# Two modulation blocks computed as columns, weights held and conditions streamed, in an adaLN transformer block on one core

## The chip, the cores and the metric

The kernel runs on one core of a Trainium2 chip. A core has five engines with instruction streams of their own: TensorE (PE in the profile; its weight loads are PEld), VectorE (DVE), ScalarE (ACT), GpSimd (POOL) and SyncE (SP, which here only issues DMA). They meet through semaphores. The metric is the device time in microseconds of one execution.

## The reference

One block with adaptive layer norm. A condition vector for each of two batches gives six modulation vectors of 512; the first two of them, `sa` and `ca`, are added to and multiplied with the normalised input ahead of the attention.

```python
mod = (silu(c) @ wmod).reshape(2, 6, 1, 512)      # c: (2, 512), wmod: (512, 3072)
sa, ca, ga, sb, cb, gb = (mod[:, i] for i in range(6))
ga, gb = sign(ga) * max(|ga|, 0.25), ...           # x: (2, 1024, 512)
h = layernorm(x) * (1 + ca) + sa
x = x + ga * attention(h)     # 32 query heads, 8 key/value heads of 128, rope, window of 128
h = layernorm(x) * (1 + cb) + sb
x = x + gb * ffn(h)           # silu gate, 512 wide, biases
```

## The kernel before, in words

All instructions of an engine run in the order in which its function writes them; waits on semaphores are written out by hand. The channels of a token lie on partitions where TensorE needs them, so the input is transposed on TensorE, tile by tile (128 tokens), and the modulation is then a scale and a shift per partition: `modT[:, kind, k, b]` holds for modulation `kind` (0 is `sa`, 1 is `1 + ca`) and channel block `k` (four of 128) one column per batch `b`.

Every matrix operand is split into two fp32r parts, a high one (ScalarE casts it) and a low one (VectorE subtracts), and a product is three matmuls of the parts (`mm3`, L276 to L278).

**The start.** SyncE and ScalarE issue the loads: the modulation weights `wm[0]` and `wm[1]` (512x512 float32 each) in halves of two channel blocks, with one semaphore a half (`s_wmk`), between them the first tiles of x into `y`, then the first weights `wk` and `wq` into the buffers `st`. `csil` is silu of the condition, transposed: 128 partitions x 4 blocks x 2 batches.

- TensorE: `mod_row(0)` and `mod_row(1)` hold the two columns of `csil` and stream 512 columns of weights, so each result is a row per batch, 2x512, in the banks `pTr` and `pAv`. Then `first_transpose(0)` and `(1)` turn two normalised tiles; `mod_columns(0)` turns the first row back into columns, four transposes into the bank `pXx`; `first_transpose(2)`, `(3)`, and `mod_columns(1)`.
- ScalarE: `row_copy(0, 0)` and `row_copy(1, 1)` copy the rows from PSUM into `crow`, which `mod_columns` reads. Behind them in its stream stand two weight casts (`split_weight`), then `first_act` of tiles 0, 2 and 3, which applies `modT`.
- VectorE: statistics and normalisation of tiles 0 to 3 (`ln_stats`, L965 to L969, and `ln_apply`, L977), `split_first(0)` and `(1)` (L1036), each of which waits for its ScalarE cast, `mod_out(0)` and `(1)` (L1090, L1092), which wait until both blocks' columns are there and write `modT`, then `first_tile` of tiles 1 (which it scales itself, L991), 0, 2 and 3: a cast (L999) and a subtraction (L1001) into `hT`.
- TensorE starts the projections when tiles 1 and 0 are in `hT` (`l_chunk0`): K and the first query head, each in two halves of 256 tokens, then the other heads and V, with the transposes of tiles 4 to 6 between them.

From there VectorE, ScalarE and GpSimd apply rope and the splits in a relay (`swap`, `rope_cos`, `rope_sin`, `rope_sum`, `rope_hi`, `rope_lo`); the other four modulation blocks are still computed as rows later on, and the loop over heads and tiles follows, with the feed-forward part at the end.

Of the kernel before, what the change touches and what calls it, by code (L numbers as in the profile page):

```python
# [24 lines left out]
P = 128  # L25
# [46 lines left out]
def adaln_block(nc, x, wq, wk, wv, wo, w12, b12, w3, b3, cond, wmod, cos, sin, x1_spill, out):  # L72
    B, SEQ, D = x.shape
# [4 lines left out]
    KT = D // P  # L78
# [7 lines left out]
    with ExitStack() as ctx:  # L86
        def sb(name, shape, dt):
            return ctx.enter_context(nc.sbuf_tensor(name, shape, dt))

        def sem(name):  # L90
            return ctx.enter_context(nc.semaphore(name))
# [8 lines left out]
        def over(name, region, offset, shape, dt):  # L100
            return nc.alloc_sbuf_tensor_at(name, shape, dt, offset=base[region] + offset)
# [23 lines left out]
        csil = sb("csil", [P, KT, B], F32)  # L125
# [10 lines left out]
        wm = [over(f"wm{i}", r, o, [P, KT, 512], F32) for i, (r, o) in enumerate(  # L136
            [("qT0", 0), ("qT0", 8192), ("wos", 0), ("qT1", 0), ("qT1", 8192), ("wos", 8192)])]
# [15 lines left out]
        pTr, pAv, pOp, pXx, pP0, pP1 = (ctx.enter_context(nc.psum_tensor(n, [P, 512], F32))  # L153
                                        for n in ("pTr", "pAv", "pOp", "pXx", "pP0", "pP1"))
# [6 lines left out]
        s_wm = [sem(f"s_wm{i}") for i in range(6)]  # L161
        s_wmk = [[sem(f"s_wmk{i}{k}") for k in range(2)] for i in range(2)]


        s_cT, s_cact, s_cdve, s_row, s_rowc, s_mod, s_modT, s_gdve, s_bias = (sem(n) for n in (
            "s_cT", "s_cact", "s_cdve", "s_row", "s_rowc", "s_mod", "s_modT", "s_gdve", "s_bias"))
# [37 lines left out]
        def l_acted(L):  # L204

            return L if L else 1
# [66 lines left out]
        def _(pe):  # L273
# [93 lines left out]
            def first_transpose(L):  # L367

                pe.wait_ge(l_norm, L + 1)
                if L in (4, 5):  # L370
                    pe.wait_ge(s_rowc, L - 3)
                if L == 6:
                    pe.wait_ge(s_modT, 1)
                if L == 7:
                    pe.wait_ge(l_act, l_acted(4))
                for k in range(KT):
                    last = nc.tensor.transpose(ln_banks[L][:, k * P:(k + 1) * P], y[:, L, k * P:(k + 1) * P], ident[:])
                last.then_inc(l_tr, 1)
# [58 lines left out]
            def mod_row(r):  # L437

                w = ROW_BLOCK[r]
                if r >= 2:  # L440
                    pe.wait_ge(s_wm[w], 16)
                if r == 3:
                    pe.wait_ge(l_act, l_acted(5))
                if r == 4:
                    pe.wait_ge(s_rowc, 3)
                if r == 5:
                    pe.wait_ge(s_modT, 2)
                for k in range(KT):
                    if r < 2 and k % 2 == 0:
                        pe.wait_ge(s_wmk[r][k // 2], 16)  # L450
                    last = nc.tensor.matmul(row_banks[r], csil[:, k, :], wm[w][:, k, :],
                                            start=(k == 0), stop=(k == KT - 1))
                last.then_inc(s_row, 1)

            def mod_columns(kind):

                pe.wait_ge(s_rowc, kind + 1)
                if kind == 2:
                    pe.wait_ge(j_done, 6)
                for k in range(KT):  # L460
                    at = 8 * kind + 2 * k
                    last = nc.tensor.transpose(pXx[:, at:at + B], crow[:, kind % 2, k * P:(k + 1) * P], ident[0:B, 0:B])
                last.then_inc(s_mod, 1)
# [2 lines left out]
            pe.wait_ge(s_c, 16)  # L466
            nc.tensor.transpose(pXx[:, 0:B * KT], c8[:], ident[0:B * KT, 0:B * KT]).then_inc(s_cT, 1)
            pe.wait_ge(s_cdve, 3)
            mod_row(0)
            mod_row(1)  # L470
            first_transpose(0)
            first_transpose(1)
            mod_columns(0)
            first_transpose(2)
            first_transpose(3)
            mod_columns(1)
            f0 = Frame(pe, 0)

            def project_half(name, half):
# [141 lines left out]
        def _(act):  # L621
            def split_weight(f, dst, W, slot):

                f.wait(w_in[slot], 32, 16 * (W // 5 + 1))
                nc.scalar.copy(dst, st[:, slot, :]).then_inc(w_hi, 1)
# [43 lines left out]
            def v_hi(f, ch, v):  # L669

                f.wait(v_turn, PER_V, v)
                nc.scalar.copy(kv[:, 0, 1, ch * CT:(ch + 1) * CT], pXx[:]).then_inc(v_half, 1)
# [34 lines left out]
            def first_act(L):  # L707

                act.wait_ge(l_tr, L + 1)
                for k in range(KT):  # L710
                    last = nc.scalar.activation(y[:, L, k * P:(k + 1) * P], ln_banks[L][:, k * P:(k + 1) * P],
                                                ACT.Identity, bias=modT[:, 0, k, 0:1], scale=modT[:, 1, k, 0:1])
                last.then_inc(l_act, 1)
# [27 lines left out]
            def unit_step(f, u, b, jobs, prev=True, prev2=True, split=True):  # L741
                if u == 2:

                    f.wait(u_scores, PER_U, u + 1)
                    splits(f, u, b)
                if prev2:
                    result_hi(f, u - 2)
                if prev:
                    p_hi(f, u - 1)
                exps(f, u)  # L750
                jobs()
                if split and u in (3, 4, 5):
                    splits(f, u, b)
# [6 lines left out]
                                 ).then_inc(s_cact, 1)  # L760

            def row_copy(r, slot):
                act.wait_ge(s_row, r + 1)
                nc.scalar.copy(crow[:, slot, :], row_banks[r]).then_inc(s_rowc, 1)

            f0 = Frame(act, 0)
            row_copy(0, 0)
            row_copy(1, 1)
            split_weight(f0, wp[:, 0, 0, :], 0, 0)
            split_weight(f0, wp[:, 0, 1, :], 1, 1)  # L770
            act.wait_ge(s_modT, 1)
# [19 lines left out]
            for b in range(B):  # L791
                s0 = b * NKV
                f = Frame(act, s0)

                def first_jobs(u):
                    if b == 0 and u == 1:
                        act.wait_ge(s_row, 5)
                    if b == 0 and u == 0:
                        first_act(7)
                        row_copy(3, 1)  # L800
                        v_hi(f, 0, 1)
                    jobs_act(f, u, b)
                for u in range(2):
                    unit_step(f, u, b, lambda: first_jobs(u), prev=s0 > 0 or u > 0, prev2=s0 > 0)
                if b == 0:
                    act.wait_ge(s_row, 6)
                else:
                    act.wait_ge(s_modT, 2)
                with nc.scalar.Fori(s0, s0 + NKV - 1) as s:
                    f = Frame(act, s, regs, s0)  # L810
                    for u in range(2, NT + 2):
                        unit_step(f, u, b, lambda: jobs_act(f, u, b, js=u // NT))
                        if u == 6:
                            side_act(f, b)
                f = Frame(act, s0 + NKV - 1)
                for u in range(2, NT):
                    def jobs():
                        if b == 0 or u < CH:
                            jobs_act(f, u, b)
                        elif u < NT - 1:  # L820
                            weight_tr_act(4 * (u - CH)), weight_tr_act(4 * (u - CH) + 1)
                    unit_step(f, u, b, jobs, split=b == 0)
                    if u == 6:
                        side_act(f, b)
                    if b == 1 and CH <= u < NT - 1:
                        weight_tr_act(4 * (u - CH) + 2), weight_tr_act(4 * (u - CH) + 3)
# [33 lines left out]
        def _(dve):  # L860
# [245 lines left out]
            def gate_row(gate):  # L1106

                bank, g = row_banks[4 + gate], grow[:, gate, :]
                dve.wait_ge(s_row, gate + 5)
                nc.vector.tensor_scalar(g, bank, 0.0, 0.5, ALU.is_ge, ALU.subtract).then_inc(s_gdve, 1)  # L1110
                dve.wait_ge(s_gdve, 3 * gate + 1)
                nc.vector.scalar_tensor_tensor(out=gmag[:], in0=g, scalar=4.0, in1=bank, op0=ALU.mult,
                                               op1=ALU.mult).then_inc(s_gdve, 1)
                dve.wait_ge(s_gdve, 3 * gate + 2)
                nc.vector.scalar_tensor_tensor(out=g, in0=gmag[:], scalar=2 * MIN_GATE, in1=g, op0=ALU.max,
                                               op1=ALU.mult).then_inc(s_gdve, 1)
# [119 lines left out]
            for h in range(2):  # L1236
                n = slice(256 * h, 256 * h + 256)
# [387 lines left out]
```

## Time and profile before

| | |
|---|---|
| median of 3 runs | 1498.3 us (1497.09, 1498.3, 1499.03) |
| profiled execution | 1499.11 us, span 1497.3 us |
| TensorE busy | 1474.5 us, 98% of the span |
| VectorE, GpSimd, ScalarE busy | 1102.8, 863.2, 823.0 us |
| mean granted clock of TensorE | 0.997 |
| first projection starts | 21.57 us after the span's start |

The busy share is over the whole span; the first 60 us look different from the rest and are read on their own. The granted clock is a share of 2.4 GHz: 1.00 is 2.4 GHz, 0.50 is 1.2 GHz. Times within the trace count from the span's first instruction.

### The profile page before, as it was taken

The numbers are of one execution on the slowest core, as the hardware profiler recorded it, in microseconds if no ns is written. First come the engines' busy times: TensorE is split into PE (matmuls) and PEld (weight loads), VectorE is DVE, ScalarE is ACT, GpSimd is POOL, SyncE is SP. The second block draws the span as 40 slices with busy tenths as digits, with TensorE's granted clock in tenths as the row PEclk, the third lists the DMA queues.
The fourth block names the chain that finished last, engine by engine and source line by source line (L and its number), as shares of the span: only waits on it lengthen the run. The fifth ranks groups of instructions, "written<-read, shape, count | busy, mean of one in ns | idle before, by whom it ended". The sixth has DMA issues, their size and how long they took to land.

```text
span 1497.3 us, 27356 instructions
## 1 busy us (share of the span) xinstructions
PE 1474.5 (98%) x7589; PEld 1227.1 (82%) x7589; DVE 1102.8 (74%) x1852; ACT 823.0 (55%) x2183; POOL 863.2 (58%) x887
## 2 busy tenths in 40 slices
PE   7899999999999999999999999999999999999999
PEld 4578888888888888888888888888888888877887
DVE  6687786877787878788787878787877868783542
ACT  3465655656555656555565655565665556552331
POOL 2356466656565556669855646655664665676333
PEclk9999999999999999999999999999999999999999
DMA  9011110110201111324302020111111101153001
GB/s 317 21 37 57 36 56 28 38 53 7 84 7 56 35 56 35 127 62 128 99 27 66 7 82 9 56 35 56 35 56 35 56 28 35 64 183 127 28 29 57
DMA packets 99216, 90.20 MB, mean 60 GB/s; under 512 B 5466, under 2 KB 73314, under 8 KB 99174
## 3 DMA queue, kind: packets, MB, share of 16 engines
q1 hardware_dynamic: 98582, 88.50, 18.8%
q10 hardware_dynamic: 432, 0.66, 0.1%
q0 software_dynamic: 160, 0.52, 0.1%
q8 instruction: 21, 0.34, 0.1%
q14 instruction: 21, 0.17, 0.0%
HBM read 74.98 MB, written 14.69 MB: 60 GB/s over the span
## 4 chain that ended last, share of the span: by engine, by line
PE 91%; DVE 4%; POOL 2%; issue 1%; ACT 1%; DMA 0%; DVEq 0%; POOLq 0%; ACTq 0%
PE pP L276 11%; PE pP L278 11%; PE pP L277 11%; PE pOp L276 8%; PE pOp L278 8%; PE pOp L277 8%; PE pS L278 4%; PE pS L277 4%; PE pAv L276 4%; PE pS L276 4%; PE pAv L278 4%; PE pAv L277 4%; PE pTr L286 3%; PE pXx L355 1%; POOL pm L1256 1%
## 5 line engine op out<-in xcount | busy, mean ns | idle before, releaser
L1256 POOL TENSOR_SCALAR_AFFINE_SELECT pm<-pT 128x512 fp32r<-128x512 f32 x480 | 393.3, 852 | 474.4 <-DVE pT L868 474.2
L276 PE MATMUL pP<-hT,wp 128*128 128x512 f32 (+1 forms) x776 | 315.1, 406 | 4.7 <-DVE hT L1001 4.0
L278 PE MATMUL pP<-hT,wp 128*128 128x512 f32 (+1 forms) x776 | 303.7, 391 | 0.0
L277 PE MATMUL pP<-hT,wp 128*128 128x512 f32 (+1 forms) x776 | 302.8, 390 | 0.0
L630 ACT CAST oT<-pAv 128x512 fp32r<-128x512 f32 x128 | 74.8, 585 | 280.9 <-PE pAv L278 280.9
L1269 POOL TENSOR_TENSOR rB<-rB,tab 128x512 f32<-128x512 f32 x160 | 218.4, 1377 | 17.3 <-ACT rB L653 17.3
L642 ACT ACTIVATE pr<-pS,nb 128x128 f32<-128x128 f32 x512 | 181.4, 371 | 64.3 <-DVE nb L888 64.3
L898 DVE TENSOR_TENSOR rA<-pP,tab 128x512 f32<-128x512 f32 x160 | 110.2, 689 | 130.8 <-ACT rB L653 130.8
L276 PE MATMUL pOp<-wos,oT 128*128 128x512 f32 x512 | 201.4, 393 | 4.0 <-DVE oT L863 3.8
L278 PE MATMUL pOp<-wos,oT 128*128 128x512 f32 x512 | 199.5, 390 | 0.0
L277 PE MATMUL pOp<-wos,oT 128*128 128x512 f32 x512 | 199.4, 389 | 0.0
L278 PEld LDWEIGHTS pP<-hT,wp 128*128 128x128 f32 x776 | 147.4, 190 | 32.0
L276 PEld LDWEIGHTS pP<-hT,wp 128*128 128x128 f32 x776 | 147.6, 190 | 30.7 <-DVE hT L1001 4.1
L277 PEld LDWEIGHTS pP<-hT,wp 128*128 128x128 f32 x776 | 148.1, 191 | 26.6
L915 DVE TENSOR_TENSOR qT<-rA,qT 128x512 fp32r<-128x512 f32 x128 | 135.3, 1075 | 19.3 <-ACT qT L662 19.3
L1263 POOL TENSOR_TENSOR pr<-pr,rs 128x512 f32<-128x512 f32 x128 | 139.3, 1088 | 15.7 <-DVE rs L893 15.7
L276 PE MATMUL pS<-kv,qT 128*128 128x192 f32 (+2 forms) x512 | 141.4, 276 | 0.1
L278 PE MATMUL pS<-kv,qT 128*128 128x192 f32 (+2 forms) x512 | 140.8, 275 | 0.0
L277 PE MATMUL pS<-kv,qT 128*128 128x192 f32 (+2 forms) x512 | 140.2, 274 | 0.0
L904 DVE TENSOR_TENSOR rA<-rA,rB 128x512 f32<-128x512 f32 x160 | 132.5, 859 | 0.0
L652 ACT COPY rB<-pP 64x512 f32<-64x512 f32 x160 | 93.5, 584 | 62.5 <-PE pP L278 60.1
L276 PEld LDWEIGHTS pOp<-wos,oT 128*128 128x128 f32 x512 | 96.1, 188 | 30.0 <-issue 5.7
(196 smaller groups left out, 3008.6 us busy)
## 6 DMA issues: line engine op xcount, KB each, us to landing
st<-in_L_attn_wq_dram SPq DMA_DIRECT2D x64, 256.0 KB, 3.6
st<-in_L_attn_wo_dram SPq DMA_DIRECT2D x64, 256.0 KB, 3.8
h_dram<-hs SPq DMA_DIRECT2D x16, 512.0 KB, 3.9
st<-in_L_attn_wk_dram SPq DMA_DIRECT2D x16, 256.0 KB, 4.0
st<-in_L_attn_wv_dram SPq DMA_DIRECT2D x16, 256.0 KB, 2.8
wm<-in_L_wmod_dram SPq DMA_DIRECT2D x4, 1024.0 KB, 10.1
xin<-in_L_attn_x_dram SPq DMA_DIRECT2D x16, 256.0 KB, 3.0
qT<-h_dram SPq DMA_DIRECT2D x2, 2048.0 KB, 10.2
```

The lines of the kernel that those rows point to most:

```text
L276: nc.tensor.matmul(o, hi_l, hi_r, start=start, stop=False, skip_group_check=True)
L277: nc.tensor.matmul(o, hi_l, lo_r, start=False, stop=False, skip_group_check=True)
L278: return nc.tensor.matmul(o, lo_l, hi_r, start=False, stop=stop, skip_group_check=True)
L630: nc.scalar.copy(oT[:, 0].rearrange("p h q -> p (h q)"), pAv[:]).then_inc(u_ohi, 1)
L642: last = nc.scalar.activation(pr[:, u % 2, i, :], pS[:, at:at + P], ACT.Exp, bias=nb[:, u % 2, i:i + 1], scale=SCALE, accum_out=sums[:, u ...
L652: nc.scalar.copy(rB[0:64, r, :], pP[j % 2][64:128, :])
L898: nc.vector.tensor_tensor(rA[:, j % 3, :], pP[j % 2][:], tab[:, 0, ch * CT:(ch + 1) * CT], ALU.mult).then_inc(r_cos, 1)
L904: nc.vector.tensor_tensor(rA[:, j % 3, :], rA[:, j % 3, :], rB[:, j % 3, :], ALU.add).then_inc(r_sum, 1)
L915: nc.vector.tensor_tensor(dst, src, hi, ALU.subtract).then_inc(j_done, 1)
L1256: last = nc.gpsimd.affine_select(out=pm[:, own, part], in_=pT[:, part], compare_op=op, fill=0.0, base=0, pattern=[[0, G], [sign, P]], chan ...
L1263: nc.gpsimd.tensor_tensor(pr[:, u % 2], pr[:, u % 2], rs[:, u % 2, :].unsqueeze(2).to_broadcast([P, G, P]), ALU.mult).then_inc(u_norm, 1)
L1269: nc.gpsimd.tensor_tensor(rB[:, j % 3, :], rB[:, j % 3, :], tab[:, 1, ch * CT:(ch + 1) * CT], ALU.mult).then_inc(r_sin, 1)
```

## The change

`mod_row` no longer computes blocks 0 and 1. `mod_direct` does: for each of the four input blocks k and four output blocks n it holds a 128x128 piece of the modulation weights and streams the two columns of `csil`, accumulating over k straight into the columns of `pXx` that `mod_out` reads. The rows, their two copies on ScalarE and the eight column transposes go away. Both blocks are computed ahead of the four tile transposes, which were mixed with the column transposes before. The remaining waits on row counts are renumbered, and the waits of tiles 4 and 5 on the row copies go, since the banks `pTr` and `pAv` no longer hold rows 0 and 1.

```diff
             def first_transpose(L):
 
                 pe.wait_ge(l_norm, L + 1)
-                if L in (4, 5):
-                    pe.wait_ge(s_rowc, L - 3)
                 if L == 6:
                     pe.wait_ge(s_modT, 1)
...
             def mod_row(r):
 
                 w = ROW_BLOCK[r]
-                if r >= 2:
-                    pe.wait_ge(s_wm[w], 16)
+                pe.wait_ge(s_wm[w], 16)
                 if r == 3:
                     pe.wait_ge(l_act, l_acted(5))
                 if r == 4:
-                    pe.wait_ge(s_rowc, 3)
+                    pe.wait_ge(s_rowc, 1)
                 if r == 5:
                     pe.wait_ge(s_modT, 2)
                 for k in range(KT):
-                    if r < 2 and k % 2 == 0:
-                        pe.wait_ge(s_wmk[r][k // 2], 16)
                     last = nc.tensor.matmul(row_banks[r], csil[:, k, :], wm[w][:, k, :],
                                             start=(k == 0), stop=(k == KT - 1))
                 last.then_inc(s_row, 1)
 
+            def mod_direct(kind):
+
+                for k in range(KT):
+                    if k % 2 == 0:
+                        pe.wait_ge(s_wmk[kind][k // 2], 16)
+                    for n in range(KT):
+                        at = 8 * kind + 2 * n
+                        last = nc.tensor.matmul(pXx[:, at:at + B], wm[kind][:, k, n * P:(n + 1) * P], csil[:, k, :],
+                                                start=(k == 0 and n == 0), stop=(k == KT - 1),
+                                                skip_group_check=True)
+                last.then_inc(s_mod, 1)
+
             def mod_columns(kind):
 
-                pe.wait_ge(s_rowc, kind + 1)
+                pe.wait_ge(s_rowc, kind - 1)
...
             pe.wait_ge(s_cdve, 3)
-            mod_row(0)
-            mod_row(1)
-            first_transpose(0)
-            first_transpose(1)
-            mod_columns(0)
-            first_transpose(2)
-            first_transpose(3)
-            mod_columns(1)
+            mod_direct(0)
+            mod_direct(1)
+            for L in range(4):
+                first_transpose(L)
             f0 = Frame(pe, 0)
...
             def row_copy(r, slot):
-                act.wait_ge(s_row, r + 1)
+                act.wait_ge(s_row, r - 1)
                 nc.scalar.copy(crow[:, slot, :], row_banks[r]).then_inc(s_rowc, 1)
 
             f0 = Frame(act, 0)
-            row_copy(0, 0)
-            row_copy(1, 1)
             split_weight(f0, wp[:, 0, 0, :], 0, 0)
             split_weight(f0, wp[:, 0, 1, :], 1, 1)
             act.wait_ge(s_modT, 1)
```

On TensorE, at the start of the program, behind the transposition of the condition, the difference reads as follows (`wm_49` and `wm_50` are the two weight blocks; the operand named first behind the arrow is the one streamed for the rows, `wm`, and the one held is `csil`; the shape is that of the output).

```order
-L451 MATMUL pTr<-wm_49,csil 2x512 x4
-L451 MATMUL pAv<-wm_50,csil 2x512 x4
-L377 MATMUL pP<-ident,y 128x128 x8
-L462 MATMUL pXx<-ident,crow 128x2 x4
-L377 MATMUL pS<-ident,y 128x128 x8
-L462 MATMUL pXx<-ident,crow 128x2 x4
+L457 MATMUL pXx<-csil,wm_49 128x2 x16
+L457 MATMUL pXx<-csil,wm_50 128x2 x16
+L375 MATMUL pP<-ident,y 128x128 x8
+L375 MATMUL pS<-ident,y 128x128 x8
```

Eight row products and eight column transposes become 32 products of two columns, and the sixteen tile transposes (four tiles) stand behind them in one piece.

On ScalarE, from the start of the program to the first application of `modT`, this stood before:

```order
L759 ACTIVATE cT<-pXx 128x8
L764 COPY crow<-pTr 2x512
L764 COPY crow<-pAv 2x512
L625 CAST wp<-st 128x512 x2
L711 ACTIVATE y<-pP,modT 128x128 x4
L711 ACTIVATE y<-pS,modT 128x128 x8
L625 CAST wp<-st 128x512
```

and this stands there now:

```order
L762 ACTIVATE cT<-pXx 128x8
L628 CAST wp<-st 128x512 x2
L714 ACTIVATE y<-pP,modT 128x128 x4
L714 ACTIVATE y<-pS,modT 128x128 x8
L628 CAST wp<-st 128x512
```

The two weight casts no longer stand behind the row copies. The orders of VectorE, GpSimd and SyncE are as they were.

## Rows read from the trace of the kernel before

**Rows 1.** The page: busy times, and the chain's shares by engine
```profile
PE 1474.5 (98%) x7589; PEld 1227.1 (82%) x7589; DVE 1102.8 (74%) x1852; ACT 823.0 (55%) x2183; POOL 863.2 (58%) x887
...
PE 91%; DVE 4%; POOL 2%; issue 1%; ACT 1%; DMA 0%; DVEq 0%; POOLq 0%; ACTq 0%
```

**Rows 2.** A window of the body: busy by engine, clock, DMA share, GB/s
```profile
800.00:1200.00 400.00, 400.00 (x2104) 338.51 (x2103) 310.12 (x523) 236.67 (x641) 233.82 (x241) 1.00 0.14 43
```

**Rows 3.** The chain of waits, 0 to 60 us: start, us, what
```profile
0.82 4.06 DMA wm<-in_L_wmod_dram
...
5.01 6.42 PE pTr L451 x8
11.44 3.43 PE pAv L451 x8
14.87 1.03 PE pP L377 x8
...
17.25 0.35 PE pXx L462 x4
...
17.90 1.38 DVE y L991 x4
...
21.57 0.58 PE pP L276
...
22.37 0.21 PE pP L278
...
28.64 0.12 PE pP L277
```

**Rows 4.** Windows of the start, same columns (busy in turn of PE, PEld, DVE, ACT, POOL)
```profile
40.40:44.30 3.90, 0.00 (x0) 0.00 (x0) 3.83 (x8) 1.48 (x4) 2.26 (x2) 1.00 0.22 67
...
44.80:48.20 3.40, 3.40 (x11) 2.64 (x10) 3.33 (x7) 0.62 (x1) 2.24 (x2) 0.51 0.00 0
...
21.50:27.70 6.20, 6.12 (x28) 6.13 (x29) 5.55 (x14) 1.20 (x3) 1.33 (x2) 0.50 1.05 386
```

**Rows 5.** Line L451, 0 to 30 us: ns min/median/max, first and last start
```profile
L451 PEld LDWEIGHTS pTr<-wm,csil x8: 80/129/129, 5.0 to 10.1; 128*2 128x2 f32 x8
L451 PE MATMUL pTr<-wm,csil x8: 593/1061/1061, 5.0 to 10.8; 128*2 128x512 f32 x8
L451 PEld LDWEIGHTS pAv<-wm,csil x8: 85/85/86, 10.8 to 13.9; 128*2 128x2 f32 x8
L451 PE MATMUL pAv<-wm,csil x8: 592/592/592, 11.3 to 14.3; 128*2 128x512 f32 x8
```

**Rows 6.** Timeline of TensorE's loads at the first column transposes
```profile
15.83 0.32 PEld L462 LDWEIGHTS pXx<-ident,crow 2*128 2x128 f32 x4 [0.17 <-issue]
```

**Rows 7.** Line L462, 0 to 30 us
```profile
L462 PEld LDWEIGHTS pXx<-ident,crow x8: 133/136/138, 15.8 to 17.4; 2*128 2x128 f32 x8
L462 PE MATMUL pXx<-ident,crow x8: 195/196/218, 15.8 to 17.4; 2*128 2x2 f32 x8
```

**Rows 8.** DMA issues at 2.84, 4.5 and 5.0 us: size, us to landing
```profile
wm<-in_L_wmod_dram SPq DMA_DIRECT2D x1, 512.0 KB, 7.5
...
st<-in_L_attn_wk_dram SPq DMA_DIRECT2D x1, 256.0 KB, 8.1
...
st<-in_L_attn_wq_dram SPq DMA_DIRECT2D x1, 256.0 KB, 8.5
```

**Rows 9.** Timelines of VectorE and of ScalarE, 14 to 19 us
```profile
14.45 0.55 DVE L977 TENSOR_SCALAR y<-y,mv 128x512 f32<-128x512 f32 x1 [0.44 <-POOL mv L1281]
16.04 1.29 DVE L1036 TENSOR_TENSOR wp<-st,wp 128x512 fp32r<-128x512 f32 x2 [1.04 <-ACT wp L625]
17.63 0.17 DVE L1090 COPY modT<-pXx 128x8 f32<-128x8 f32 x1 [0.29 <-PE pXx L462]
...
15.39 1.13 ACT L625 CAST wp<-st 128x512 fp32r<-128x512 f32 x2
...
19.28 2.90 ACT L711 ACTIVATE y<-pS,modT 128x128 f32<-128x128 f32 x8
```

More of the change, by code:

```diff
@@ L796, in first_jobs @@
                     if b == 0 and u == 1:
-                        act.wait_ge(s_row, 5)
+                        act.wait_ge(s_row, 3)
                     if b == 0 and u == 0:
@@ L805, in _ @@
                 if b == 0:
-                    act.wait_ge(s_row, 6)
+                    act.wait_ge(s_row, 4)
                 else:
@@ L1108, in gate_row @@
                 bank, g = row_banks[4 + gate], grow[:, gate, :]
-                dve.wait_ge(s_row, gate + 5)
+                dve.wait_ge(s_row, gate + 3)
                 nc.vector.tensor_scalar(g, bank, 0.0, 0.5, ALU.is_ge, ALU.subtract).then_inc(s_gdve, 1)
```

## The prediction

> **What bounds the kernel now.** I began with the page: TensorE is busy for 98% of the span and carries 91% of the chain that ended last, VectorE only 4% [rows 1]. The windows over the body say the same: from 60 us on TensorE has no hole worth naming [rows 2]. So nothing in the body changes, and whatever the start gains or loses in reaching that body reaches the end one for one. The change touches only the first 18 us.
>
> Next the chain of waits at the start [rows 3]. It runs from the landing of the first half of the first modulation block (0.82 + 4.06 = 4.9) over the two row products on TensorE (6.42 and 3.43 us), the transposes of four tiles with the eight small column transposes between them (to 17.25 + 0.35 = 17.60), and then VectorE: shift and scale of tile 1 from 17.90, and the splitting of tiles 1 and 0. There the first projection starts, at 21.57. Behind it TensorE works until the relay of ScalarE, VectorE and GpSimd through rope makes it wait once more, 40.4 to 44.3 [rows 4], and then it is the bound.
>
> **What the change does to TensorE.** Removed: 16 instructions of 512 streamed columns and 8 column transposes. The rows cost 6.42 + 3.43 = 9.85 us, the columns 2 x 0.35 = 0.70 [rows 3]. The first eight row instructions were at TensorE's lower level (1061 ns each, 1.2 GHz), the second eight at the higher (592 ns, 2.4 GHz) [rows 5]. Added: 2 blocks x 4 k x 4 n = 32 products. The trace shows each float32 product as two instructions (x8 where the program has four) [rows 5], so 64 pairs of a 128-column weight load and a 2-column stream.
>
> No row has that very pair. The nearest is the column transpose: 128 columns held, 2 streamed, at the high level. Four loads are busy for 0.32 us together [rows 6], each 0.136 [rows 7], so they start (0.32 - 0.136) / 3 = 0.061 us apart; on the chain a group of four takes 0.35, 0.088 each [rows 3]. At the low level I allow twice either: 0.12 to 0.18 us. Below, the bound is 0.061; above, it is the whole load without any overlap. That load at the low level: a 2-column load takes 85 ns high and 129 low [rows 5], a 128-column one 136 high [rows 7], so 126 columns cost 51 ns high, 102 low, together 0.231. I take 0.14, between the two readings of the nearest row, and the low level throughout, since nothing shows whether this work raises the clock. Then the blocks last 64 x 0.14 = 9.0 us, from 5.0 to 14.0.
>
> The weights arrive in time: the last half block is issued at about 2.8 and takes 7.5 us, so it lands at about 10.3 [rows 8], when three quarters of the pairs (5.0 + 48 x 0.14 = 11.7) aren't yet done. With pairs at 0.061 this landing would set the end instead: 10.3 + 16 x 0.061 = 11.3.
>
> Behind the blocks stand the four tile transposes. Eight took 1.03 us at the high level [rows 3], so at the low level tiles 0 and 1 are through at 14.0 + 2.1 = 16.1.
>
> **What waits for it.** On ScalarE the copy of the second row, which waited for the product's end, held the first weight split back to 15.39 [rows 9]. Both copies go. The split then waits for its data: wk was issued at about 4.5 and takes 8.1, so it lands at 12.6, wq at 5.0 + 8.5 = 13.5 [rows 8]. The splits take 1.13 us together [rows 9], so the second is done by about 14.1.
>
> VectorE's order isn't changed. It normalises tile 3 until 14.45 + 0.55 = 15.00, then idled 1.04 us for the split, did its two halves in 1.29 us, idled 0.29 for the columns and wrote modT [rows 9]. Now the first idle goes (the splits are there at 14.1), and the second too (the blocks end at 14.0). So VectorE: 15.0 + 0.02, + 1.29 = 16.3, and with the two small operations at the old spacing (17.63 to 17.90, 0.27) the shift of tile 1 starts at 16.6 instead of 17.90. TensorE has tile 1 ready at 16.1. **The gain is 1.04 + 0.29 = 1.3 us**, not the several us that TensorE saves: VectorE's tile statistics and splits are the next thing late, and hide the rest. ScalarE starts tile 0 at the same moment. Tiles 2 and 3 are transposed by 14.0 + 4.1 = 18.1, before ScalarE comes to tile 3, two tiles of 1.45 us after 16.6 [rows 9].
>
> Everything behind moves by 1.3 us: the projection starts at about 20.3. The loads that SyncE issues when VectorE frees a weight buffer come 1 us earlier, and TensorE waits for none of them: its one long wait behind the projection's start is that for VectorE until 44.3. The removed waits of tiles 4 and 5 cost nothing now, for those tiles stand behind the projections. Were VectorE's work out of the way, TensorE would set the start: tile 1 is through at 16.1, so at these prices there are only 0.5 us more behind it.
>
> **The clock.** It was low over the first 6.2 us of the projection, after TensorE had stood idle from 17.60 to 21.57 [rows 3, 4]; it was low again from 44.8 to 48.2, behind the idle 3.9 us that ended at 44.3 [rows 4]. Low, a projection step is 0.21 us, high 0.12 [rows 3]. In the new order the idle time before the projection is longer, so it starts low again; I take the same low stretch. If it lasted only 3.4 us, as the other did, 2.8 us fewer would be worth 2.8 x (1 - 0.12 / 0.21) = 1.2 us; if the second fall didn't come, 3.4 x (1 - 0.12 / 0.21) = 1.5.
>
> **Sum.** The profiled execution took 1499.1 us (its span of 1497.3 and 1.8 around it); 1499.1 - 1.3 = 1497.8. It was 0.8 above the median of 1498.3, and 1499.03 and 1497.09 are among the three runs: executions differ by as much as the change is worth. Against the median I forecast 1497.0.
>
> **The rivals.**
> *A, the pairs don't overlap (slower).* A load can't start under the last matmul, and the clock stays low: 64 x 0.231 = 14.8, blocks to 19.8, tiles 0 and 1 to 21.9, shift of tile 1 at 22.0 instead of 17.90: +4.1 us, 1502.4. For it: the loads are 128 columns wide and nothing else is in the stream, and the high level came only after 5.8 us of wide products, 5.0 to 10.8 [rows 5]. Against it: the 0.061 spacing of loads 0.136 long [rows 6, 7]. It decides from a pair of (17.9 + 3.0 - 2.1 - 5.0) / 64 = 0.216 us on. Chance 0.08.
>
> *B, pairs of 0.15 to 0.21 us.* From (16.6 - 2.1 - 5.0) / 64 = 0.149 on TensorE is late again. At 0.175 the start is 5.0 + 11.2 + 2.1 = 18.3, a loss of 0.4; at 0.20 a loss of 2.0. Time 1497.5 to 1501, chance 0.2.
>
> *C, the clock gives back as well.* 1.3 + 1.2 + 1.5 = 4.0 us: 1494.3. For it: both falls follow idle stretches of about 3.9 us, and both shift. Against it: neither idle stretch gets shorter. Chance 0.12 for a gain of over 3 us, which needs most of both.
>
> *D, loads wait for the matmul's full duration.* Each pair would then take 0.136 + 0.196 = 0.332 us even at the high level [rows 7], 64 of them 21.2 us; blocks to 26.2, shift of tile 1 at 27.3, +9.4 us, 1507.7. Against it: four such pairs take 0.35 us on the chain [rows 3], where it would give 1.33. Chance 0.02.
> The Trainium skill ("TensorE: Matmul & The Clock Gate", Part 3, "The mechanism") states this rule: a weight load overlaps a matmul in flight only if the two use different row groups, and all loads here use all rows. The trace of the column transposes does not agree with it.
>
> *E, the forecast*, 0.58.
>
> **Numbers.** A change of under 0.2% (3.0 us) is about what a measurement of this kernel can't tell from none. Faster by more: C, 0.12. Slower by more: A and D, 0.10. Within: 0.78. The range leaves out D, A and the far end of C: with B's upper end and the spread of the runs, 1494.6 to 1499.9.
>
> **What the changed profile would show.** 64 load and stream pairs on pXx between 5.0 and about 14, 0.12 to 0.18 us apart, with at most a short wait for the last half block; no row copies before the first split, which starts at about 12.6; no idle time of VectorE between 15.0 and modT at about 16.4; the first projection at about 20.3; TensorE's second long wait ending at about 43.0; the body unchanged. It is wrong if modT waits for TensorE, if tile 1's shift waits for its transpose, or if the first projection's low stretch differs by several us from 6.2.

## The result, and the profile after

The changed kernel is slower: 1501.21 us median (1500.17 to 1502.51, 14 runs) against 1498.22 (1497.09 to 1499.03, 14 runs), a ratio of 1.002 with the 95% interval 1.0013 to 1.0027. The forecast was 1497.0, within 1494.6 to 1499.9. Run again later beside other kernels it gave 1501.86 against 1498.74, 1.0023 (1.0013 to 1.0032). One execution of all, among the eleven with the third block's row product in the idle time, took 5973.57 us and is left out of that run's median and ratio.

The page of the changed kernel, in the lines that answer to [rows 1]:

```profile
span 1499.7 us, 27432 instructions
...
PE 1479.1 (99%) x7629; PEld 1240.0 (83%) x7629; DVE 1103.1 (74%) x1852; ACT 822.2 (55%) x2181; POOL 863.2 (58%) x887
```

The page says that TensorE's busy time grew by 4.6 us, though the change was to relieve it, and that VectorE's did not change. Where it grew stands in the chain of waits (start, us, what), beside [rows 3]:

```profile
0.82 3.78 DMA wm<-in_L_wmod_dram
4.73 13.78 PE pXx L457 x64
18.52 1.82 PE pP L375 x8
20.44 1.38 DVE y L992 x4
...
24.11 0.58 PE pP L276
24.70 0.21 PE pP L277
...
31.23 0.58 ACT rB L655
...
46.64 0.91 PE pXx L375 x4
```

Two row products of 9.85 us became 64 pairs of 13.78 us, and eight tile transposes that took 1.03 us take 1.82. Tile 1's shift starts at 20.44 instead of 17.90, 2.5 us late, the projection at 24.11 instead of 21.57, the copy of the K bank (ScalarE, L655, the first work on the projection's result) at 31.23 instead of 28.91, and the span is 2.4 us longer. So the start's shift did reach the end nearly one for one.

The products' line and the tile transposes' line (ns min/median/max, first and last start), beside [rows 5] and [rows 7]:

```profile
L457 PEld LDWEIGHTS pXx<-csil,wm x64: 287/333/333, 4.7 to 18.1; 128*128 128x128 f32 x64
L457 PE MATMUL pXx<-csil,wm x64: 343/353/353, 4.7 to 18.2; 128*128 128x2 f32 x64
```

```profile
L375 PEld LDWEIGHTS pP<-ident,y x8: 224/230/370, 18.2 to 19.7; 128*128 128x128 f32 x8
L375 PE MATMUL pP<-ident,y x8: 421/421/454, 18.4 to 19.9; 128*128 128x128 f32 x8
```

The loads are 333 ns long but for the first. 64 of them follow each other every (13.73 - 0.333) / 63 = 0.213 us, 13.73 being their joint busy time in the timeline, so each starts under the one before. That is 256 cycles at 1.2 GHz: two cycles for each of the 128 held columns. The transpose's load, also of 128 columns, is 230 ns here, 103 less: about one cycle a column less. Both lines are at the low level from the first to the last instruction, to nearly 22 us, where the kernel before had risen at 10.8.

The trace of the kernel before has loads of 128 columns for products too, which [rows 5] to [rows 7] don't show. These are the projection's at the low level and at the high one, and two successive loads of the scores (start, us), at the high level, with 64 columns streamed behind each:

```profile
L276 PEld LDWEIGHTS pP<-hT,wp x6: 330/330/330, 22.2 to 25.4; 128*128 128x128 f32 x6
...
L276 PEld LDWEIGHTS pP<-hT,wp x9: 186/187/192, 29.0 to 34.7; 128*128 128x128 f32 x9
...
52.88 0.19 PEld L277 LDWEIGHTS pS<-kv,qT 128*128 128x128 f32 x1
52.99 0.19 PEld L278 LDWEIGHTS pS<-kv,qT 128*128 128x128 f32 x1
```

They belong to products of fp32r parts, one instruction a product, but the load is as long as that of the new pairs (330 against 333 ns), and the scores' loads start 0.11 us apart at the high level, which is half of 0.213.

What waited for TensorE, on VectorE and on ScalarE, beside [rows 9]:

```profile
14.80 1.28 DVE L1037 TENSOR_TENSOR wp<-st,wp 128x512 fp32r<-128x512 f32 x2
18.55 0.17 DVE L1091 COPY modT<-pXx 128x8 f32<-128x8 f32 x1 [2.46 <-PE pXx L457]
18.64 0.16 DVE L1093 TENSOR_SCALAR modT<-pXx 128x8 f32<-128x8 f32 x1
20.44 1.37 DVE L992 TENSOR_SCALAR y<-pP,modT 128x128 f32<-128x128 f32 x4 [1.65 <-PE pP L375]
```

```profile
12.50 0.62 ACT L628 CAST wp<-st 128x512 fp32r<-128x512 f32 x1 [9.10 <-DMA st<-in_L_attn_wk_dram]
13.37 0.62 ACT L628 CAST wp<-st 128x512 fp32r<-128x512 f32 x1 [0.25 <-DMA st<-in_L_attn_wq_dram]
19.57 1.50 ACT L714 ACTIVATE y<-pP,modT 128x128 f32<-128x128 f32 x4 [5.59 <-PE pP L375]
```

The casts moved up to the landing of their weights, as forecast, and VectorE's splits run on from its last normalisation. Then VectorE waits twice for TensorE: 2.46 us for the blocks, 1.65 us for tile 1. Both waits were to be nothing.

One reading needs care. A window of the changed kernel over its first projection (busy times of PE, PEld, DVE, ACT, POOL, then granted clock, DMA, GB/s):

```profile
24.10:30.20 6.10, 6.08 (x30) 6.09 (x31) 5.45 (x13) 0.52 (x2) 1.33 (x2) 1.00 1.05 386
```

The column says 1.00, but the steps in it are 0.21 us apart, the low level's distance; so it does in the first microseconds of every kernel here. At the start the level is read from the durations.

### The profile page after: what moved, and what is told of

It is laid out like the page before. It is cut to its first block, busy times and chain, and to the rows that moved or that the text cites. A ratio compares the mean times of both kernels' runs of the same rounds, so it can differ in the third digit from the quotient of the medians.

```text
span 1499.7 us, 27432 instructions
## 1 busy us (share of the span) xinstructions
PE 1479.1 (99%) x7629; PEld 1240.0 (83%) x7629; DVE 1103.1 (74%) x1852; ACT 822.2 (55%) x2181; POOL 863.2 (58%) x887
## 4 chain that ended last, share of the span: by engine, by line
PE 91%; DVE 4%; POOL 2%; issue 1%; ACT 1%; DMA 0%; DVEq 0%; POOLq 0%; ACTq 0%
PE pP L276 11%; PE pP L278 11%; PE pP L277 11%; PE pOp L276 8%; PE pOp L278 8%; PE pOp L277 8%; PE pS L278 4%; PE pS L277 4%; PE pAv L276 4%; PE pS L276 4%; PE pAv L277 4%; PE pAv L278 4%; PE pTr L286 3%; PE pXx L457 1%; PE pXx L355 1%
## 5 line engine op out<-in xcount | busy, mean ns | idle before, releaser
L655 ACT COPY rB<-pP 64x512 f32<-64x512 f32 x160 | 93.4, 584 | 62.9 <-PE pP L278 60.5
## 6 DMA issues: line engine op xcount, KB each, us to landing
wm<-in_L_wmod_dram SPq DMA_DIRECT2D x4, 1024.0 KB, 10.8
```

What stands on the lines that cost most here:

```text
L655: nc.scalar.copy(rB[0:64, r, :], pP[j % 2][64:128, :])
```

## The experiments

Two questions were open: what a pair costs, and why the clock stayed low. Each run below is compared with the kernel before on the same chip.

**64 columns streamed.** The loads are the same, but more columns go through them. The results go to the banks `pTr` and `pAv`, from which `mod_out` reads the first two of each 64 columns, and tiles 4 and 5 wait for `modT`, because they use the same banks; of the edit only the product is shown.

```diff
-                        at = 8 * kind + 2 * n
-                        last = nc.tensor.matmul(pXx[:, at:at + B], wm[kind][:, k, n * P:(n + 1) * P], csil[:, k, :],
+                        last = nc.tensor.matmul((pTr, pAv)[kind][:, 64 * n:64 * (n + 1)],
+                                                wm[kind][:, k, n * P:(n + 1) * P],
+                                                csil[:, k, :].unsqueeze(1).to_broadcast([P, 32, B]),
```

> Each of the 64 loads is followed by a stream of 64 columns (the two condition columns repeated 32 times, the copies going to spare columns of the banks pTr and pAv) in place of 2; the loads, their order and the result are the same. Theory 1 (the loss is the clock: two-column streams leave TensorE at its low level, where a load pair costs 0.215 us): the clock rises at about 10.5 to 11, as it did under the row products; from there a pair takes about half, 0.11 us, the blocks end at about 14.5 instead of 18.5, the tile transposes are at the high level, VectorE's shift of tile 1 starts at about 16.6 to 17, and the kernel takes 1496 to 1498 us, 3 to 4 less than the changed kernel. Rival 2 (a pair costs 0.215 us whatever the clock, say in the sequencer): the pairs stay at 0.215 us, the end at 18.5, and only the transposes get faster: 1500 to 1501. Rival 3 (the clock doesn't rise on this work, however wide): as the changed kernel or slower, 1501 to 1502.

Measured: 1501.98 us against 1498.74, 1.0024 (1.0014 to 1.0034). The loads of both blocks:

```profile
L456 PEld LDWEIGHTS pTr<-csil,wm x32: 289/333/337, 5.1 to 11.7; 128*128 128x128 f32 x32
L456 PEld LDWEIGHTS pAv<-csil,wm x32: 333/333/333, 11.9 to 18.5; 128*128 128x128 f32 x32
```

Nothing moved: the loads are at the low level to the end of the blocks, at the same distance. The 62 extra columns cost no time, so the stream lies wholly beside the loads. Theory 1 as I had put it (a wider stream brings the clock up) failed here. Whether the stream was still too small, or the clock wasn't to be moved, this run can't say; and as the clock never rose, rival 2 (0.215 us at any clock) isn't tested by it either.

**128 columns streamed.** The same edit with 128 for 64 and 64 for 32.

> As the run with 64 streamed columns, now 128 (the two condition columns 64 times over), so that the stream takes as long as the load, 256 cycles each. With 64 columns the pairs stayed at 0.216 us and the clock stayed low. If it is the share of time in which columns stream that raises the clock (in the row products they stream nearly all the time), it now rises at about 10.5 to 11, the later pairs take half, the blocks end at about 14.7, and the kernel takes 1496 to 1498 us. Rival (load and stream of such a product don't overlap): pairs of 0.32 to 0.43 us, blocks beyond 25, 1508 or more. Rival (it stays low whatever is streamed): as the changed kernel, 1501.

Measured: 1497.28 us against 1498.24, 0.9992 (0.9983 to 1.0001). Loads, streams, and VectorE's start:

```profile
L456 PEld LDWEIGHTS pTr<-csil,wm x32: 190/333/333, 4.9 to 10.6; 128*128 128x128 f32 x32
L456 PE MATMUL pTr<-csil,wm x32: 272/421/553, 4.9 to 10.8; 128*128 128x128 f32 x32
L456 PEld LDWEIGHTS pAv<-csil,wm x32: 191/191/192, 10.8 to 14.2; 128*128 128x128 f32 x32
```

```profile
14.85 1.29 DVE L1038 TENSOR_TENSOR wp<-st,wp 128x512 fp32r<-128x512 f32 x2
16.05 0.16 DVE L1095 COPY modT<-pTr 128x8 f32<-128x8 f32 x1
16.13 0.16 DVE L1097 TENSOR_SCALAR modT<-pAv 128x8 f32<-128x8 f32 x1
16.32 1.37 DVE L993 TENSOR_SCALAR y<-pP,modT 128x128 f32<-128x128 f32 x4
```

The first block's loads are 333 ns long but for the last ones, the second's all 191: the high level came at 9.7, near the end of the first block. In the second block 32 loads are busy for 3.65 us (the timeline's figure), so they start (3.65 - 0.191) / 31 = 0.112 us apart, half of 0.213 and a few ns, so a price of 0.215 us at any clock is out. The last load ends at 14.4, no wait is left between VectorE's splits and tile 1's shift, and that starts at 16.32, 4.1 us ahead of the changed kernel and 1.6 ahead of the kernel before. With this one number altered, the start of the changed kernel goes as the prediction said. The gain on the kernel before lies just inside what the runs can't tell from none; the interval doesn't touch that of the changed kernel (1.0013 to 1.0032).

**64 columns held.** Half of each output block is left out of the computation, so the result is incomplete and only the trace counts. One more transposition of the condition stands ahead of it and writes columns 8 to 15 of `pXx`.

```diff
-                        last = nc.tensor.matmul(pXx[:, at:at + B], wm[kind][:, k, n * P:(n + 1) * P], csil[:, k, :],
+                        last = nc.tensor.matmul(pXx[0:64, at:at + B], wm[kind][:, k, n * P:n * P + 64], csil[:, k, :],
...
+            nc.tensor.transpose(pXx[:, B * KT:2 * B * KT], c8[:], ident[0:B * KT, 0:B * KT])
             nc.tensor.transpose(pXx[:, 0:B * KT], c8[:], ident[0:B * KT, 0:B * KT]).then_inc(s_cT, 1)
```

> Each product of the two blocks holds 64 columns of weights instead of 128 (the upper half of each output block is left out of the computation). Theory 1 (the pair is the load, two cycles per held column at 1.2 GHz: 128 x 2 / 1.2 = 213 ns): a pair takes about 0.11 us at the low level and the blocks are bound by the landing of the last half block at 10.3, ending at about 12. Rival 2 (a fixed cost per pair): pairs stay at 0.215 us and the blocks end at about 18.5.

Measured: 1497.36 us, a single execution. From the timeline:

```profile
4.63 1.78 PEld L457 LDWEIGHTS pXx<-csil,wm 128*64 128x64 f32 x16 [1.99 <-DVE swapped L1077]
...
7.03 5.19 PEld L457 LDWEIGHTS pXx<-csil,wm 128*64 128x64 f32 x48 [0.62 <-DMA wm<-in_L_wmod_dram]
```

The median load is 227 ns, so 48 of them start (5.19 - 0.227) / 47 = 0.106 us apart, half of 0.213. A pair costs its held columns, two cycles each at 1.2 GHz, and next to nothing besides; a fixed cost is out. The wait in it is for the second half block's weights, not for the last as expected: the last 48 loads run on without one. The clock stayed low under the blocks here too, and it didn't matter: they end at 12.2, tile 1's shift starts at 16.11. So halving the load and doubling the clock are worth about the same, and either makes VectorE the one to wait for.

**Block 0 as a row, block 1 directly.** The counts that the waits on rows and their copies use are set to match; that part of the edit isn't shown.

```diff
-            mod_direct(0)
+            mod_row(0)
             mod_direct(1)
+            mod_columns(0)
```

> Block 0 as a row (its copy and its four column transposes with it), block 1 directly, then the transposes of tiles 0 to 3. The row product brings the clock up by 10.5 to 11, so block 1's pairs run at the high level. If the pair is the load of 256 cycles, they take 0.107 us there (32 in 3.4 us, ending at about 14.7), the tile transposes are at the high level, VectorE runs through from 15.0, tile 1's shift starts at about 16.7, and the kernel gains the 1.3 us that the prediction forecast: 1497. If the pair costs 0.215 us at any clock, block 1 ends at 18.2 and the kernel takes 1500 or more.

Measured: 1498.43 us against 1498.24, 1.0000 (0.9991 to 1.0009). Windows over block 1 and over the tile transposes (columns as above), and VectorE's start:

```profile
12.50:13.50 1.00, 1.00 (x11) 1.00 (x11) 0.93 (x5) 0.64 (x2) 0.45 (x1) 1.00 1.07 361
...
14.50:15.00 0.50, 0.50 (x4) 0.50 (x3) 0.50 (x2) 0.00 (x0) 0.00 (x0) 0.50 1.04 382
...
17.00:18.00 1.00, 1.00 (x6) 1.00 (x6) 0.00 (x0) 0.48 (x2) 0.00 (x0) 0.50 1.09 348
```

```profile
14.91 1.28 DVE L1044 TENSOR_TENSOR wp<-st,wp 128x512 fp32r<-128x512 f32 x2
16.40 0.17 DVE L1098 COPY modT<-pXx 128x8 f32<-128x8 f32 x1 [0.20 <-PE pXx L474]
...
18.39 1.36 DVE L999 TENSOR_SCALAR y<-pP,modT 128x128 f32<-128x128 f32 x4 [1.74 <-PE pP L377]
```

The pair is about 0.11 us at the high level, as expected, for the first 25 loads (starts from 11.5 to 14.2). Then came what I had not expected: the granted clock fell to 0.50 by 14.5, while TensorE was busy all through the windows around it, with nothing but these pairs since 11.5. The tile transposes ran low, tile 1's shift waited 1.74 us for them, and the gain was gone. So it isn't only that this work can fail to raise the clock; here the clock fell under it. The place is seen in one trace, but the mean granted clock of all eleven executions (0.994 to 0.995) is below the 0.997 that nearly all of the kernel before show.

**Tile 0 between the blocks.**

```diff
             mod_direct(0)
+            first_transpose(0)
             mod_direct(1)
-            for L in range(4):
+            for L in range(1, 4):
```

> The changed kernel with tile 0's transposes between the two blocks, the rest of the order as it is. If the order matters only by the time that TensorE needs behind the blocks for tiles 0 and 1 (0.23 us a transpose at the low level, 1.9 us for eight), tile 1 is through 0.9 us earlier only if its own transposes come first; here the last block ends 0.9 us later (19.4) and tile 1 at the same time as before, about 20.4: no change, 1501. Rival (VectorE could start 1 us earlier because tile 0 is off the path): 1500.

Measured: 1502.14 us against 1498.74, 1.0024 (1.0014 to 1.0033).

```profile
20.71 1.37 DVE L993 TENSOR_SCALAR y<-pP,modT 128x128 f32<-128x128 f32 x4 [0.80 <-PE pP L375]
```

Tile 1's shift starts no earlier, as expected; this order gives nothing, and TensorE's own work sets the start. Moving tile 1's transposes themselves ahead of the last pairs was not tried. This trace shows one thing more, which bears on the clock: the projection's steps are at the high level from its first at 24.39, though TensorE had stood idle for 2.1 us before and no filler was there, and the K bank's copy starts at 29.00. The execution took 1501.32 us all the same; the low level came later and lasted from 43.3 to 50.1.

**The kernel before, with casts and columns first.** Rows as they were.

```diff
             row_copy(0, 0)
-            row_copy(1, 1)
             split_weight(f0, wp[:, 0, 0, :], 0, 0)
             split_weight(f0, wp[:, 0, 1, :], 1, 1)
+            row_copy(1, 1)
...
             mod_columns(0)
+            mod_columns(1)
             first_transpose(2)
             first_transpose(3)
-            mod_columns(1)
```

> The kernel before, rows and all, with two moves: ScalarE's two weight casts ahead of the second row's copy, and the second block's column transposes ahead of the transposes of tiles 2 and 3. If what the start waits for in the kernel before is VectorE behind those casts and columns, VectorE runs through from 15.0, modT is there at about 16.7 in place of 17.9 and the kernel gains 1.0 to 1.3 us: about 1497.1. Rival (the gain is lost again, in the clock's low stretch or in the relay to 44 us): 1498.2, as before.

Measured: 1497.6 us against 1498.74, 0.9995 (0.9986 to 1.0004). Tile 1's shift starts at 16.17:

```profile
14.70 1.28 DVE L1036 TENSOR_TENSOR wp<-st,wp 128x512 fp32r<-128x512 f32 x2
15.90 0.16 DVE L1090 COPY modT<-pXx 128x8 f32<-128x8 f32 x1
...
16.17 1.36 DVE L991 TENSOR_SCALAR y<-pP,modT 128x128 f32<-128x128 f32 x4
```

No wait is printed between VectorE's splits and tile 1's shift, as with 128 streamed columns. All that the change could have given at this place in the trace comes from the order of ScalarE's and TensorE's instructions, with the rows kept. The median is 1.1 us lower, in line with it, but the interval takes in no gain at all.

**The third block's row product in TensorE's idle time,** on top of the last one.

```diff
+                if name == "Q3":
+                    mod_row(2)
                 if name != "V":
                     first_transpose(2 + j)
-            mod_row(2)
```

> The rows version with casts and columns first (its profile's TensorE idle from about 38.7 to 42.6), and the row product of the third block (3.5 us) moved from behind the V projection into that idle time, ahead of tile 6's transposes. If TensorE's own work bounds everything behind the idle time, 3.5 us go, and if the fall of the clock behind it comes from the idle time, another 1.5: 1492 to 1494 us. Rival (something else releases the scores at 51, or the block's weights are late): 1496 to 1497.5.

Measured: 1499.0 us (median of ten) against 1498.24, 1.0006 (0.9997 to 1.0016). The 1492 to 1494 expected are missed: no gain, and if anything a loss. Windows:

```profile
40.00:44.00 4.00, 3.59 (x16) 1.99 (x14) 3.93 (x8) 1.78 (x3) 2.03 (x2) 1.00 0.00 0
44.00:48.00 4.00, 1.30 (x6) 0.75 (x4) 3.32 (x6) 1.89 (x4) 1.80 (x2) 0.98 0.00 0
48.00:52.00 4.00, 3.29 (x16) 3.29 (x16) 2.92 (x6) 4.00 (x12) 0.00 (x0) 0.50 0.01 2
```

and, in the chain of waits, the last link of the relay ahead of TensorE:

```profile
47.96 0.70 DVE qT L916
```

The idle time moved from before 44 to behind it: the scores wait for the relay, which VectorE's rope of the last query head ends only at 48.7. They do start earlier, at 48.71 against 51.06 in the run that this one builds on, but the clock was low behind this idle time too, to 54.7, where the other trace is at the high level from 46.5 on, and the lead was gone. In the kernel before, the relay ends at 51.2 and TensorE's row product stands from 49.25 to 52.77, so it covered that wait. The prediction's view that TensorE is the bound from 44.3 on therefore held only because the row product stood where it did.

**The filler, and two last versions.** Eight row products into a bank that nobody reads, behind tile 3's transposes, first on top of the last run, then on the version with 128 streamed columns and on the rows version with casts and columns first:

```diff
+            for k in range(KT):
+                nc.tensor.matmul(row_banks[2], csil[:, k, :], wm[1][:, k, :], start=(k == 0), stop=(k == KT - 1))
             f0 = Frame(pe, 0)
```

> The same, and eight row products of 512 columns whose result nobody reads put between tile 3's transposes and the first projection, about 16.5 to 19.9, where TensorE was idle. If the low level in the first projection (0.21 us a step instead of 0.12, over some 6 us) comes from that idle time, the K bank is done 2 to 2.8 us earlier and the kernel gains up to 2.4 us more: 1490 to 1492. Rival (the relay behind it is bound by VectorE's own work, or the clock falls anyway): as the run without the filler.

> The direct products with 128 streamed columns, and the eight unread row products of 512 columns behind tile 3's transposes, about 16.3 to 19.8. Theory (the first projection's low level comes from TensorE's idle time before it): the clock is high when the projection starts at about 20, the K bank is done some 2 us earlier than without the filler (26.1), and the kernel gains about 2 us on the 128-column run, 3 on the kernel before: 0.998, or 1495 us where the kernel before takes 1498. Rival (the relay of VectorE behind it takes up the gain): 0.9992, as without the filler.

> The rows version with casts and columns first, with the same filler and without the move of the third block's row product. If that move was what cost the earlier run its gain (1 to 2 us lost against the version without it), this one takes 0.998 of the kernel before, level with the direct version with filler, since both start tile 1's shift at about 16.2 to 16.3: how the columns are computed makes no difference once VectorE is the one to wait for. Rival (the direct version is better by the copies and column transposes that it saves): this one is over 1 us slower than the direct version with filler.

> The changed kernel once more, beside the others on this chip: 1.002 of the kernel before, the 64 pairs 0.215 us apart at the low level to 18.5, and tile 1's shift at 20.4.

Measured: on top of the moved row product 1496.4 against 1498.24, 0.9990 (0.9981 to 0.9999), where 1490 to 1492 had been expected; with 128 streamed columns 1495.55 against 1498.74, 0.9983 (0.9974 to 0.9992); with rows 1495.98, 0.9983 (0.9974 to 0.9992). The changed kernel, on the chip of the last two: 1501.86, 1.0023. Windows over the place of the filler and over the projection, first without it (128 columns), then with it:

```profile
16.40:19.90 3.50, 0.00 (x0) 0.00 (x0) 3.40 (x9) 3.50 (x11) 0.00 (x0) 1.00 1.14 323
20.00:26.80 6.80, 6.80 (x44) 6.80 (x45) 5.48 (x13) 1.84 (x5) 1.33 (x2) 0.75 1.06 380
```

```profile
16.30:20.00 3.70, 3.70 (x15) 1.10 (x13) 3.56 (x11) 3.48 (x11) 0.00 (x0) 1.00 1.15 324
20.00:26.80 6.80, 6.52 (x50) 5.82 (x48) 6.08 (x15) 2.98 (x7) 1.75 (x3) 1.00 1.06 380
```

With the filler the clock stays high through the projection, in all three traces that have one, and the copy of the K bank starts 4.6 us behind the projection's start instead of 6.1 (25.12 - 20.50 against 26.08 - 20.00). What the filler itself gives is seen best in the two runs on the same chip that differ in nothing else: 1499.0 us without and 1496.4 with it, on top of the moved row product, and nine of the ten executions without it took longer than the longest with it. So the relay doesn't take up all of the gain. With 128 streamed columns the filler's share is less sure: the two ratios to the kernel before, 0.9992 and 0.9983, have intervals that overlap, and the K bank was done 1.0 us earlier, not 2. Both last versions beat both kernels, by 3.2 and 2.8 us on the kernel before and by about 6 on the changed one, and they are level with each other, as expected, with tile 1's shift at 16.52 and 16.70: rows or columns makes no difference once VectorE is the one to wait for.

The changed kernel's second trace, with the start of the projection in two windows:

```profile
5.14 13.79 PE pXx L457 x64
...
20.86 1.38 DVE y L992 x4
```

```profile
24.50:26.00 1.50, 1.47 (x12) 1.47 (x13) 1.43 (x4) 0.55 (x2) 0.00 (x0) 1.00 1.05 386
26.10:29.30 3.20, 3.20 (x17) 3.20 (x16) 3.06 (x9) 0.00 (x0) 0.56 (x2) 0.50 1.06 387
```

The pairs cost the same to a hundredth, and tile 1's shift is 0.4 us later because the blocks' start is. But the projection began at the high level here and was low from 26.0 to 29.4 only, 3.4 us instead of nearly 6. How much of the projection runs low thus differs between executions of one kernel. Idle time ahead of the projection isn't enough for a low start, by this trace and by that with tile 0 between the blocks; without the idle time none of three was low.

## Why the prediction was wrong

- **The step that failed: "I take 0.14, between the two readings of the nearest row".** The pair costs 0.213 us at the low level. The nearest row was that of a transpose, and a transpose's load takes about one cycle a held column where that of a product takes two. The same row fits for how loads follow each other (0.061 us for loads of 136 ns) and misleads on how long each holds the path. The trace of before has rows for the price that the working didn't use: the projection's loads of 128 columns last 330 ns low and 187 high, and the scores' loads start 0.11 us apart high, twice of which is 0.22. That a float32 product's load would match one of fp32r parts could only be assumed then; the changed kernel shows it. The rows used for rival A give the length too, once a load of a product stands in for that of the transpose: 187 - 85 = 102 ns for 126 columns more at the high level, so 204 at the low, where the prediction had 51 and 102; with the 129 of the short load that makes 333 ns, the length measured.
- **The low level throughout the blocks** was assumed and was so. The rest of the formula holds: 4.73 + 13.78 for the blocks and 1.82 for tiles 0 and 1 give 20.3, and tile 1's shift started at 20.44. With 0.213 in place of 0.14, rival B's working gives 5.0 + 13.6 + 2.1 = 20.7, 2.8 us behind the 17.90 of before.
- **Rivals.** The outcome stands between B (0.15 to 0.21) and A (0.216 on), for a reason that is neither's: the loads do overlap, spaced 0.213 and 333 ns long, but each costs about twice what the transpose's does. That B's span of prices happened to reach to 0.21 was luck: its working had no reason for the doubling. B's own time ran to 1501, and the range was closed at 1499.9 although it claims to take in B's upper end; that sum was wrong, and the result of 1501.21 lies just above B's end. Rival D is out for these pairs as well: the matmuls take 353 ns each and don't add to the pair. With that the rule of the Trainium skill that the prediction names there ("TensorE: Matmul & The Clock Gate", Part 3, "The mechanism") doesn't hold here. The pairs are the better witness: the prediction says that all loads use all rows, but those of the column transposes have two ([rows 7]), and only the 64 pairs' loads have all 128.
- **What hides the rest.** That VectorE would be the next to wait for, and the gain of 1.3 us with it, was right as a mechanism: with 128 streamed columns, and with 64 held, VectorE shows no wait for TensorE there and tile 1's shift starts 1.6 and 1.8 us earlier than before. The changed kernel never got there; TensorE ended 4.1 us behind that point.
- **ScalarE's casts** moved to 12.50 and 13.37, forecast 12.6 and 13.5. The landings of the modulation weights held nothing up once the first was there: the 64 loads run without a gap.
- **The clock in the projection** was low for nearly 6 us in the profiled execution, as taken, and for 3.4 in the other trace of the same kernel, so the agreement is in part luck. That both low stretches come from idle time was left as a rival's ground. For the first the filler supports it, three traces of three being high; that it is the whole cause isn't shown, since the projection also began high twice behind 2.1 us of idle time. The second, behind 44, stayed in every version.
- **The sum.** The start is 2.5 us late in the profile and the span 2.4; the medians differ by 3.0. The runs of one kernel spread over 2 us, and where that last half microsecond comes from isn't settled. TensorE's second long wait ended at 46.64, 2.3 us later than before, where 43.0 was forecast: the start's shift was carried on to it.

## What to carry to other kernels

Swapping the held and the streamed operand trades streaming for loading, and in float32 a load cost two cycles a held column here, with 2 and with 64 columns behind it. Count the loads in the trace, not the products in the program: each float32 product is two instructions, so 2 x 128 x 2 cycles for one that holds 128 columns (0.43 us at 1.2 GHz), at the level of the clock at that place. Take the price of a load from a product, not from a transpose, and search the whole trace for one that holds as many columns. Products that load much and stream little can also leave TensorE at its low level, and whatever stands behind them pays; before rebuilding such a piece, look who waits for whom, for here two moved calls brought tile 1's shift as far forward as any version with direct products, though their gain in time was too small to be told from none.

## What the runs showed of the hardware that was not expected

- Under 64 pairs with 2 and with 64 streamed columns TensorE was busy for 13.8 us without a gap and stayed at 1.2 GHz to their end; under the same loads with 128 streamed columns it rose at 9.7 in one trace and at 10.9 in the other, under row products at 10.8 in the kernel before. After a row product had raised it, it fell again by 14.5 under pairs with 2 columns, begun at 11.5, with no idle time.
- Loads of 128 columns for a float32 product start 0.213 us apart at the low level, 0.112 at the high; of 64 columns, 0.106 at the low. A float32 transpose's load of 128 columns is 230 ns long at the low level where the product's is 333; a load for fp32r products is 330 ns there, like the float32 one.
- The profile's column of the granted clock reads 1.00 at the start whatever the level, and in the changed kernel's profiled execution up to 30 us; durations tell it.
